# A graph layer on one Trainium2 core: warm-up transposes and split sample loads in the front, the last octet's scores, softmax and pooling rescheduled in the tail

## What is computed

```python
def _mab(x, y, in_w, in_b, out_w, out_b, ff_w, ff_b, y_mask=None):
    q, k, v = ...                       # x and y times the three parts of in_w
    s = einsum('bqd,bkd->bqk', q, k) / sqrt(d)       # masked slots: -inf
    h = softmax(s) @ v @ out_w + out_b + x
    return h + relu(h @ ff_w + ff_b)
h = x @ w_lin + b_lin
dense = rows h[edge_src] of each node's first 32 edges     # (n, 32, 64)
xb = _mab(dense, dense, enc..., mask)
xp = relu(xb @ pma_lin_w + pma_lin_b)
p = _mab(seed, xp, pma..., mask)        # one row per node
dd = _mab(p, p, dec...)
x = layernorm(x + relu(nan_to_num(dd)))
```

## Time and profile before

| | us |
|---|---|
| median of 3 runs | 4012.61 (4012.59 to 4014.58) |
| the profiled execution | 4014.11 |
| its span in the trace | 4012.3 |
| busy: PE, DVE, POOL, ACT | 3111.6, 3057.7, 2979.5, 1663.4 |
| gathers of table rows | 3093, 949 ns each |

### The profile page before, as it was taken

The page is one execution under the profiler, slowest core; times in us unless marked ns, Lnnn a source line. Parts: engine busy times, 40 slices in busy tenths (PEclk is TensorE's granted clock), DMA queues, the critical chain, the costliest instruction groups (busy, mean ns, idle before and its releaser), DMA issues.

```text
span 4012.3 us, 111968 instructions
## 1 busy us (share of the span) xinstructions
PE 3111.6 (78%) x30804; PEld 2000.9 (50%) x30804; DVE 3057.7 (76%) x7192; ACT 1663.4 (41%) x3006; POOL 2979.5 (74%) x3145
## 2 busy tenths in 40 slices
PE   7877887877777778777787787787877777877777
PEld 5544554554545445545454455454554554545443
DVE  6877877877778768777787787777877877778876
ACT  3443443444434434444444344344444443434443
POOL 6777777777777777777777777777777777777772
PEclk8999998999989989999899899998999999999898
DMA  6333333333333333333333333333333333333331
GB/s 215 90 90 90 90 91 90 90 91 89 90 90 89 91 90 89 90 90 90 90 89 90 90 89 91 90 90 90 89 91 90 90 90 90 90 90 89 87 109 34
DMA packets 186843, 369.25 MB, mean 92 GB/s; under 512 B 66610, under 2 KB 119002, under 8 KB 186090
## 3 DMA queue, kind: packets, MB, share of 16 engines
q0 software_dynamic: 150080, 307.11, 28.8%
q1 hardware_dynamic: 29802, 45.03, 3.5%
q10 hardware_dynamic: 6208, 8.40, 0.7%
HBM read 347.48 MB, written 16.32 MB: 91 GB/s over the span
## 4 chain that ended last, share of the span: by engine, by line
POOL 66%; issue 24%; PE 6%; DVE 2%; DMA 1%; POOLq 1%; SPq 0%; ACT 0%; DVEq 0%
POOL gathered L620 66%; DMA gathered<-node_table,idx 1%; PE ps L788 1%; PE ps L726 1%; PE ps L738 1%; PE ps L770 1%; PE ps L801 0%; DVE windows L1135 0%; PE ps L815 0%; PE ps L831 0%; PE ps L762 0%; POOLq L131 0%; DMA node_table<-gathered 0%; PE ps L689 0%; DVE probs_diag L1382 0%
## 5 line engine op out<-in xcount | busy, mean ns | idle before, releaser
L620 POOL DMA_INDIRECT gathered<-node_table,idx x3093 | 2934.4, 949 | 943.3 <-issue 938.7
L726 PE MATMUL ps<-ident,gathered 128*128 128x128 f32 x3128 | 583.5, 315 | 458.2 <-DMA gathered<-node_table,idx 452.3
L726 PEld LDWEIGHTS ps<-ident,gathered 128*128 128x128 f32 x3128 | 485.1, 203 | 796.0 <-issue 732.2
L852 ACT ACTIVATE h_apart<-ps 64x512 f32<-64x512 f32 x782 | 462.3, 591 | 448.9 <-PE ps L726 355.3
L925 ACT ACTIVATE qT<-ps,cols 128x512 f32<-128x512 f32 x391 | 268.8, 687 | 854.3 <-PE ps L726 754.4
L1306 DVE SCALAR_TENSOR_TENSOR xb<-ps,cols,h 128x512 f32<-128x512 f32 x391 | 292.1, 747 | 417.6 <-PE ps L788 412.4
L1382 DVE STREAM_TRANSPOSE probs_diag<-probs 32x512 f32<-32x512 f32 x784 | 549.0, 700 | 18.4
L738 PE MATMUL ps<-probs_diag,gathered 128*64 128x128 f32 x6256 | 462.4, 292 | 107.4 <-issue 106.1
L788 PE MATMUL ps<-h,ff_diag 128*128 128x512 f32 x782 | 484.0, 705 | 76.0 <-DVE h L1262 75.5
L738 PEld LDWEIGHTS ps<-probs_diag,gathered 128*64 128x64 f32 x6256 | 373.9, 169 | 276.8 <-issue 259.1
L852 ACT ACTIVATE xp_rows<-ps 128x512 f32<-128x512 f32 x391 | 233.4, 597 | 601.0 <-PE ps L762 419.6
(11 more groups left out here) (205 smaller groups left out, 3287.2 us busy)
## 6 DMA issues: line engine op xcount, KB each, us to landing
windows<-win_table SPq DMA_DIRECT2D x8960, 2.8 KB
gathered<-node_table,idx POOLq DMA_INDIRECT x3093
windows<-win_table ACTq DMA_DIRECT2D x2944, 2.8 KB
node_table<-gathered SPq DMA_DIRECT2D x24, 384.0 KB, 2.8
out_rows<-rows SPq DMA_DIRECT2D x5, 416.0 KB
win_table<-in_dst SPq DMA_DIRECT2D x1, 1716.0 KB
win_table<-in_src SPq DMA_DIRECT2D x1, 1716.0 KB
rows<-in_x SPq DMA_DIRECT2D x2, 640.0 KB, 5.1
```

The costliest lines, as they stand in the source:

```text
L620: pool.indirect_dma_start(out=gathered[:, s.slot(0, RING), t * ROW:(t + 1) * ROW], out_offset=None, in_=table, in_offset=bass.IndirectOffs ...
L726: mm = pe.transpose(ps[:, bank, p * P:(p + 1) * P], gathered[:, s.slot(0, RING), lo:lo + 2 * ROW - 2:3], ident[:, :])
L852: return nc.scalar.activation(o, i, ACT.Copy)
```

## The change

- **Front, PE.** `WARM` = 12 transposes of `ident` into bank 0 are issued once POOL's constants are there, before the wait for the samples.
- **Front, samples.** The load of the samples is split in two halves of 25 rows, one issued by SP, the other by ACT ahead of `FIRST_LOADS`. DVE waits for both.
- **Front, DVE.** The conversion of `iota_j` and the two sets of `node_f` instructions move from behind the diagonal multiplies to a place ahead of the wait for the samples.
- **Tail, last batch.** `s.alone()` is the straight-line step 391, the first without a new octet. There the scores of octet 390 are made right behind the attend in place of at the end of the step, and DVE does mask, add, top and subtract at the end of step 391 (behind the second half of the diagonal blocks, ahead of the statistics and the pooling sum) in place of step 392; the exponential moves to ACT's step 391, and the division and the diagonal blocks from step 393 to 392.
- **Tail, last iteration.** `LAST_SOONER` moves the seed softmax, weights, pooling, decoder and output row of iteration 97 one step forward (`sooner`).
- **Tail, bank.** The pooling of iteration 97, its transposed weights and its decoder results lie in bank 0 (`B_Q`) in place of bank 6, and its pooling matmul doesn't wait for `y_ok`.

The looped steps issue the same instructions in the same order. The core of the diff:

```diff
+WARM = 12
+LAST_SOONER = {L_SEED: 1, L_SEED_T: 1, L_WEIGHTS: 1, L_POOL: 1, L_DEC1: 1, L_DEC2: 1, L_OUT: 1, L_Y: 1}
...
+    def sooner(self, lag):
+        if self.looped or lag not in LAST_SOONER:
+            return 0
+        last = (self.octets - 1) // 4 * 4
+        return LAST_SOONER[lag] if self.at - lag + LAST_SOONER[lag] == last else 0
...
+    def alone(self, after=0):
+        return not self.looped and self.at == self.octets + after
...
+        def pool_bank(s, lag):
+            return B_Q if not s.looped and s.iteration(lag) == ITS - 1 else B_POOL
...
-            sp.dma_start(sample_i[:, :], dst.rearrange("(p k n) -> p k n", k=SAMPLE_TILES, n=STRIDE)[:, :, 0],
+            sp.dma_start(sample_i[0:SAMPLE_ROWS // 2, :], sampled_dst[0:SAMPLE_ROWS // 2, :],
                          allow_slow_non_contiguous=True).then_inc(samples_in, 16)
...
+            pe.wait_ge(pool_cst, POOL_CONSTS)
+            for i in range(WARM):
+                pe.transpose(ps[:, 0, 0:P], ident[:, :], ident[:, :])
             pe.wait_ge(samples_sb, 1)
             spread(0, 512)
             pe.wait_ge(w_first, 16 * len(FIRST_LOADS))
-            pe.wait_ge(pool_cst, POOL_CONSTS)
...
                     mm.then_inc(av_ps, 1)
+                if s.alone():
+                    scores(s)
                 if s.has_iteration(L_DEC1):
...
-                    wait(pe, y_ok, s.iteration(L_POOL))
+                    if pool_bank(s, L_POOL) == B_POOL:
+                        wait(pe, y_ok, s.iteration(L_POOL))
...
-                if s.has_batch(L_SCORES):
+                if s.has_batch(L_SCORES) and not s.alone():
+                    scores(s)
...
+            act.dma_start(sample_i[SAMPLE_ROWS // 2:SAMPLE_ROWS, :], sampled_dst[SAMPLE_ROWS // 2:SAMPLE_ROWS, :],
+                          allow_slow_non_contiguous=True).then_inc(samples_in, 16)
             for d_, s_ in FIRST_LOADS:
...
-                if s.has_batch(L_SOFTMAX):
-                    wait(act, s_diff, s.batch(L_SOFTMAX) + 1)
+                if s.alone() or s.has_batch(L_SOFTMAX) and not s.alone(1):
+                    wait(act, s_diff, s.batch(L_SOFTMAX - s.alone()) + 1)
...
             dve.wait_ge(pool_cst, POOL_CONSTS)
-            dve.wait_ge(samples_in, 16)
+            V.tensor_copy(iota_j[:, :], iota_ji[:, :])
+            for q in range(QUADS):
+                last = V.tensor_scalar(node_f[DEG * q:DEG * q + DEG, :], node_i[DEG * q:DEG * q + DEG, :],
+                                       float(-(QUADS * DEG - 1) * FULL * q), None, ALU.add)
+            link(last)
+            for q in range(QUADS):
+                last = V.tensor_scalar(node_f[DEG * q:DEG * q + DEG, FULL:ITS], node_i[DEG * q:DEG * q + DEG, FULL:ITS],
+                                       float(-(P - 1) * q), None, ALU.add)
+            link(last)
+            dve.wait_ge(samples_in, 32)
             link(V.tensor_copy(sample_f[:, :], sample_i[:, :]))
...
+                if s.has_batch(L_SOFTMAX) and not s.alone(1):
+                    masked(s, L_SOFTMAX)
+                if s.has_batch(L_NORM) and not s.alone(2):
+                    shared_out(s, L_NORM)
+                if s.alone(1):
+                    shared_out(s, L_NORM - 1)
...
+                if s.has_batch(L_NORM) and not s.alone(2):
+                    to_diagonal(s, L_NORM, QUADS // 2, QUADS)
+                if s.alone(1):
+                    to_diagonal(s, L_NORM - 1, QUADS // 2, QUADS)
+                if s.alone():
+                    masked(s, L_SOFTMAX - 1)
+                    from_top(s, L_SOFTMAX - 1)
                 if s.has_iteration(L_Y):
                     y_stats(s)
```

More of the change, by code:

```diff
@@ L98, in iteration @@
     def iteration(self, lag):
-        return self.group * (PERIOD // 4) + (self.at - lag) // 4
+        return self.group * (PERIOD // 4) + (self.at - lag + self.sooner(lag)) // 4
     def round(self, lag):
@@ L114, in has_batch @@
         return (self.at - lag) % 2 == 0 and (self.looped or 0 <= self.at - lag < self.octets)
+    def alone(self, after=0):
+        return not self.looped and self.at == self.octets + after
     def has_iteration(self, lag):
-        return (self.at - lag) % 4 == 0 and (self.looped or 0 <= self.at - lag < self.octets)
+        at = self.at - lag + self.sooner(lag)
+        if at % 4 or self.looped:
+            return at % 4 == 0
+        moved = LAST_SOONER.get(lag, 0) and at == (self.octets - 1) // 4 * 4 and not self.sooner(lag)
+        return 0 <= at < self.octets and not moved
 def wait(eng, sem, count):
@@ new lines, in step, with scores @@
+                if s.has_batch(L_SCORES) and not s.alone():
+                    scores(s)
+            def scores(s):
+                wait(pe, p_norm, s.batch(L_SCORES))
+                wait(pe, q_sb, s.octet(L_SCORES - 2))
+                wait_apart(pe, h_parted, s.octet(L_SCORES - 2) * 2, pe_passed)
+                if s.has_iteration(L_SCORES):
+                    m = s.iteration(L_SCORES)
+                    wait_apart(pe, count_ok, m + 1, pe_passed)
+                    par = s.slot(L_SCORES, PERIOD) // OCTS_PER_IT
+                    pe.matmul(ps_counts[:, 0:QUADS], fold, count_quad[:, par, :], start=True, stop=True)
+                    pe.matmul(ps_counts[:, QUADS:QUADS + 1], pool_perm, count[:, par, :], start=True, stop=True)
+                for o in range(2):
+                    for p in range(PAIRS):
+                        for q in range(QUADS):
+                            lo = p * P + DEG * q
+                            mm = pe.matmul(
+                                ps[DEG * q:DEG * q + DEG, B_S + o, 2 * DEG * p:2 * DEG * (p + 1)],
+                                qT[:, s.slot(L_SCORES - o, 4), lo:lo + DEG],
+                                h_apart[:, s.slot(L_SCORES - o, 2), p, q].rearrange("p h j -> p (h j)"),
+                                start=True, stop=True)
+                mm.then_inc(s_ps, 1)
@@ L988, in _ @@
             V.memset(eps[:, :], EPS)
[L989 to L992, removed]
-            link(last)
-            for q in range(QUADS):
-                last = V.tensor_scalar(node_f[DEG * q:DEG * q + DEG, FULL:ITS], node_i[DEG * q:DEG * q + DEG, FULL:ITS],
-                                       float(-(P - 1) * q), None, ALU.add)
-            link(last)
             PIECES = [(0, 512), (512, 1024), (1024, SAMPLES)]
@@ L1380, in to_diagonal, with first_half @@
+            def first_half(s, lag):
+                n = s.batch(lag)
+                dve.wait_ge(p_norm, n + 1)
+                wait(dve, av_ps, s.octet(lag + 2))
+                to_diagonal(s, lag, 0, QUADS // 2)
+            def to_diagonal(s, lag, first, last):
+                pr = probs[:, s.slot(lag, 4) // 2, :]
                 for q in range(first, last):
                     lo = DEG * q
-                    V.transpose(probs_diag[lo:lo + DEG, s.slot(L_NORM, 4) // 2, :, lo:lo + DEG],
+                    V.transpose(probs_diag[lo:lo + DEG, s.slot(lag, 4) // 2, :, lo:lo + DEG],
```

132 lines of the change are left out of this document (66 added, 66 removed).

## The result

| | before | after |
|---|---|---|
| median of 19 runs, us | 4013.49 (4011.7 to 4017.46) | 4021.72 (4018.43 to 4025.6) |
| the profiled execution | 4014.11 | 4020.84 |
| its span | 4012.3 | 4018.7 |
| mean granted clock of PE | 0.923 | 0.926 |

The account below looks back on a forecast made before the run. GpSimd's gathers, one every 1.25 us and untouched, bound the kernel, leaving front and tail: +1.6 + 3.2 - 1.5 + 2.2 = +5.5 us on the profiled execution, 4018.1 us on the runs' median; range 4011.5 to 4022.

Parts of the forecast that it names:

- third rival: Tail: PE's clock falls and stays low, still 0.5 at about 3980; 4020.6 to 4027 us; chance 0.14.
- Front, the moved block: Front, DVE: iota_j conversion held by POOL's memsets to 7.05 us, delaying the first index list; +1.6 us, bounds 0 and +1.6.
- a front near +0: Front: by the skill's exclusion rule DVE could get in at 5.3 us between the memsets, so almost no loss.
- Front, two queues: Front, sample load: gain 0 while the memsets cover it, at most some tenths of a us without them.
- They can only land sooner: Front: samples split over two queues arrive before 4.45 us, but nobody can use them before 7.05; gain 0.
- Front, warm-up: Front, PE: twelve transposes cost nothing and gain 0, as idle time lowers the clock again; -2.6 us if it stayed high.
- second rival: Front gains: DVE's block not held or PE warm in the spreads, -0.1 to -2.6 us; taken 4015 us; chance 0.15.
- Tail, the scores and the softmax: Tail, last batch moved up: DVE's added work and PE's waits delay attend of octet 390; +3.2 us, bounds -2.0 to +4.5.
- Tail, the clock: Tail, PE: the 3.6 us standstill lowers the granted clock, slowing later instructions; +2.2 us, between 1.3 and 3.0.
- first rival: Tail: the clock stays up in PE's standstill; 4015.9 us; chance 0.13.
- Tail, last iteration and bank: Tail: last pooling starts right behind OUT, -2.1 us, transposed weights cost 0.6; sum -1.5 us, bounds -2.1 to 0.
- signs of a wrong forecast: Fill gather before 28 us, scores without a wait for the norm, or pooled of iteration 95 less than 3 us later.

Follow-up runs that it names:

- c1: Kernel before with only the change's whole front part, tail as before; total 1.0008 of the kernel before on the same chip.
- c12: The changed kernel again, unchanged, on another chip than the first; total 1.0044 of the kernel before.
- c5: Changed kernel with the iota_j conversion and node_f sets back behind the diagonal multiplies; total 1.0013 of the kernel before.
- c7: Changed kernel with GpSimd's memsets waiting for the sample conversion and the w_lin copy behind the sample copies; total 1.0008 of the kernel before.
- c8: c7 with the last batch's scores and softmax at their old places; total 1.0006 of the kernel before.
- c9: c8 with all samples loaded by SP alone, so ScalarE's queue starts with the weights; total 1.0036 of the kernel before.
- c6: Changed kernel without the twelve warm-up transposes; total 1.0011 of the kernel before.
- c4: Changed kernel with 14 and 26 dummy transposes filling PE's two standstills in steps 391 and 392; total 1.0013 of the kernel before.
- c2: Kernel before with only the last batch's scores and softmax one step sooner; total 1.0013 of the kernel before.

## Why the prediction was right, and where it was off

The forecast was 4018.1 us with a range to 4022; measured were 4021.72. That the time lies inside the range by 0.3 us is partly luck. Of the 3.6 us between the two, 0.9 is the median of before, which rose from 4012.61 (3 runs) to 4013.49 (19); 1.2 is the profiled execution, for which the forecast said +5.5 and +6.7 came; 1.5 is not shown (below). The measured time also lies in the band of the third rival, 4020.6 to 4027. The order of the work, the waits and the place of the loss were as forecast; what was off is the size of the clock's term.

- **Front, the moved block.** +1.6 forecast, 1.56 to 1.57 measured (after, c1, c12). The held conversion is the cause: c5 takes it back by moving the block, and c7 removes the hold. The Trainium skill, "SBUF — State Buffer", "Who interferes with whom", says that cast or tensor_scalar and a GpSimd instruction exclude each other for a whole instruction. The trace agrees, but the waiting conversion was not let in where one memset followed the other at 5.3 us; a front near +0, which the prediction read out of this sentence, did not come.
- **Front, two queues.** Forecast 0 and at most a gain of some tenths. It is a cost of 0.2 (c5) that the block hid, and of 2.0 to 2.7 once the memsets are out of the way (c8 and c7 against c9). Two steps failed here, and neither reached the sum. "They can only land sooner" did not come true in any trace (4.65 to 4.68 with two queues, 4.37 to 4.66 with one). And the weights behind one more issue on ScalarE, priced at nothing, or up to 1 us without cover, made PE wait 1.56 us in c8 and 3.10 in c7.
- **Front, warm-up.** Forecast 0, measured within 0.1 in c6 against after. The first spread took 1.12 us in c7 behind 0.98 us of idle time, 1.78 in c5 behind 3.21, and 2.07 in c8 and c9 behind 0.95 and 0.67. The second rival, by which PE comes warm into the spreads, thus happens at times, and brought nothing in c5 and c7, where w_lin was waited for; what decides it is not shown.
- **Tail, the scores and the softmax.** +3.2 forecast at the attend of 390, 3.4 measured with the clock kept up (c4). pooled of iteration 95 was to come 4.5 us later and came 4.6 later there. PE's wait for pooled was to be 3.6 us and is 3.54. The reason was right as well: DVE is the busy engine here, and the work moved ahead on it delayed what stood behind it.
- **Tail, the clock.** This term was mis-sized: +2.2 forecast, 3.1 measured (28.65 against 25.53). I priced one fall, after the standstill of 3.6 us, and passed over the one of 2.2 us at the scores. The trace of before could have priced the shorter standstill too: of PE's 58 idle times of 1.75 to 2.25 us between 100 and 3900 us, 18 were followed by a fall within some 3 us. In after the first fall costs 1.5 (pooled of 95 at 15.51 against 13.97) and the second, 6.8 us long, 1.6, which is less than my 3.0 for that length. In c12 the single fall of 10.2 us costs 3.1. In c6 both came, the second 10.2 us long, and cost 5.1 together. So the third rival (+4.2 to +6 for the clock, still at 0.5 at about 3980) came true in c6, and by its sign, but not its price, in c12; in after the clock was back at 3978.6. The first rival (the clock stays up) did not happen in any of the six traces with the unfilled order (after, c2, c5, c6, c7, c12).
- **Tail, last iteration and bank.** -1.5 forecast, -1.5 measured twice.

The measured terms sum to 1.6 + 3.4 + 3.1 - 1.5 = +6.6, and the spans differ by 6.4; the sum takes the tail's terms at the attend of 390 and leaves out the -0.4 of POOL's stretch, so it agrees within some tenths. The medians differ by 8.2, which is 1.5 more than the profiled executions do: the one of before lies 0.6 above its median, the one of after 0.9 below. What makes the 1.5 is not shown. A part of the executions with the longer fall, as in c6 (1.7 more), would account for it, and the runs of after do spread more than those of before (7.2 against 5.8 us); but only one execution on the first chip has a trace.

Of the signs named beforehand all came: the iota_j conversion from 1.89 to 7.09, the spread at 9.51 in 2.07, the fill gather at 29.60, the last gather at 3949.42 (3949.8 expected), the wait for pooled (its end 23.7 us behind the last gather instead of 21, since the first fall came before it), the low clock behind it (for 5.5 us of the 10 that were named), and the last pooling matmul behind OUT. None of the signs of a wrong forecast was seen.

## What to carry to other kernels

Work moved ahead on the engine that is already busy gained nothing here, and each engine that waits for what it displaced stands still in order; price the standstill twice, once as the wait and once as the lower clock of what follows, and count every new one, not only the longest. Before moving conversions into a gap of VectorE, look at what GpSimd does there: a held instruction looks like a long one, and the gap is no gap. When a hold is removed, name the input that is late next, and keep it off the queue that the change loads.

## What was not expected of the hardware

- A standstill of PE of 2.2 us in an otherwise full stretch led to a fall of the granted clock in five traces of six (not in c12), and the low stretch lasted 3.4 us each time. After the standstill of 3.5 us it lasted 6.8 us in four and 10.2 us in two (c6, c12), with the same instructions around it.
- The same kernel ran in 4013 us on one chip and in about 6487, 6487 and 6531 us on three others. There SP issued a window load every 0.61 us instead of every 0.39, and PE stood still for 1349 to 1556 us ahead of its score matmuls without a wait that the profile shows (1.9 us on the first chip). A few microseconds gained in front or tail can't be read from total times of such a chip.
- Loading 1250 samples by two queues brought them no sooner than by one (conversion at 4.65 to 4.68 against 4.37 to 4.66); ScalarE took 1.42 us to issue its half, SP 1.03 us for its half or for the whole.
